# Router weights taken out of TensorE and multiplied in by Pool: one change to the last stage of a two-layer attention and mixture-of-experts kernel

## The reference

```
x = x + attention(layernorm(x), ctx)            # 16 heads, 154 keys
x = x + expert_choice_ffn(layernorm(x))         # 8 experts, each takes its 128 best tokens
x = x + masked_attention(layernorm(x), ctx)     # one head, mask over the keys
x = x + moe(layernorm(x))                       # 32 experts of width 64, 8 per token, and a shared one

# moe, with x of T x 128
aff   = sigmoid(x @ Wr + br)                    # T x 32
w     = aff where it is among the token's top 8, else 0; divided by its sum
gate  = silu(x @ Wg[e] + bg[e])                 # 64 units for each expert e
up    = x @ Wu[e] + bu[e]
out   = shared(x) + sum over e of w[:, e] * ((gate * up) @ Wd[e] + bd[e])
```

## Time and profile before

| what | value |
|---|---|
| time, median of 3 runs (lowest to highest) | 245.97 us (245.62 to 246.22) |
| the profiled execution, its own time | 246.02 us |
| span in the trace, first to last instruction | 244.2 us |
| so outside the span | 1.8 us |
| PE busy | 226.9 us (93%) |
| DVE busy | 180.0 us (74%) |
| ACT busy | 132.0 us (54%) |
| POOL busy | 75.1 us (31%) |
| mean granted clock of PE | 0.996 |

### The profile page before, as it was taken

The page is one execution under the profiler, slowest core; times in us unless marked ns, Lnnn a source line. Parts: engine busy times, 40 slices in busy tenths (PEclk is TensorE's granted clock), DMA queues, the critical chain, the costliest instruction groups (busy, mean ns, idle before and its releaser), DMA issues.

```text
span 244.2 us, 3720 instructions
## 1 busy us (share of the span) xinstructions
PE 226.9 (93%) x1238; PEld 157.4 (64%) x1238; DVE 180.0 (74%) x441; ACT 132.0 (54%) x267; POOL 75.1 (31%) x113
## 2 busy tenths in 40 slices
PE   8989999999997888999999998878999999999993
PEld 2446645664555334688688976646888888888871
DVE  2699887671385887898261688899888888888883
ACT  2437667779625930352443767576554554554551
POOL 6234998020412500000391112100354354354000
PEclk9999999999999999999999999999999999999998
DMA  6994000000000000000043000000111211300002
GB/s 220 399 403 155 3 0 1 3 0 0 3 0 0 0 4 1 0 0 3 1 132 86 0 3 1 0 0 3 43 43 43 86 48 43 86 0 0 3 0 86
DMA packets 5144, 11.62 MB, mean 48 GB/s; under 512 B 803, under 2 KB 1923, under 8 KB 4870
## 3 DMA queue, kind: packets, MB, share of 16 engines
q1 hardware_dynamic: 4294, 10.61, 12.9%
q10 hardware_dynamic: 832, 0.78, 1.0%
HBM read 10.87 MB, written 0.52 MB: 47 GB/s over the span
## 4 chain that ended last, share of the span: by engine, by line
PE 74%; DVE 19%; ACT 3%; issue 2%; POOL 1%; DVEq 0%; ACTq 0%; POOLq 0%
PE bank L1916 6%; PE bank L1917 5%; PE bank L1920 5%; PE bank L1414 5%; PE bank L1281 5%; PE bank L1400 4%; DVE att L686 4%; PE bank L1355 4%; PE bank L1766 3%; PE bank L1950 3%; PE bank L1953 3%; PE bank L1307 3%; PE bank L1951 3%; PE bank L1931 3%; PE bank L1753 3%
## 5 line engine op out<-in xcount | busy, mean ns | idle before, releaser
L1221 ACT ACTIVATE arena_d<-bank,bias 128x512 f32<-128x512 f32 x34 | 23.4, 688 | 32.2 <-PE bank L1920 32.2
L872 DVE SCALAR_TENSOR_TENSOR arena_d<-bank,bias,arena_d 128x512 f32<-128x512 f32 x34 | 25.5, 750 | 9.5 <-ACT arena_d L1221 9.3
L546 DVE TENSOR_REDUCE smax<-bank 128x3 f32<-128x462 f32 (+2 forms) x44 | 25.4, 620 | 5.9 <-PE bank L1355 5.6
L451 POOL CAST arena_b<-rec 128x512 fp32r<-128x512 f32 x17 | 13.4, 787 | 46.7 <-PE bank L1953 46.6
L1916 PE MATMUL bank<-arena_b 128*128 128x512 f32 x68 | 26.8, 393 | 0.1
L1920 PE MATMUL bank<-arena_b 128*128 128x512 f32 x68 | 26.6, 391 | 0.0
L1917 PE MATMUL bank<-arena_b 128*128 128x512 f32 x68 | 26.5, 390 | 0.0
L1028 ACT ACTIVATE arena_c<-bank 128x512 f32<-128x512 f32 x40 | 22.6, 597 | 7.1 <-PE bank L1400 3.3
L886 DVE TENSOR_TENSOR arena_a<-arena_d,arena_a 128x512 fp32r<-128x512 f32 x34 | 23.5, 691 | 0.8 <-ACT arena_a L1228 0.7
L1228 ACT CAST arena_a<-arena_d 128x512 fp32r<-128x512 f32 x34 | 20.8, 612 | 3.4 <-DVE arena_d L881 3.1
L881 DVE TENSOR_TENSOR arena_d<-arena_d,bank 128x512 f32<-128x512 f32 x32 | 21.8, 682 | 0.4 <-PE bank L1931 0.3
(11 more groups left out here) (252 smaller groups left out, 490.9 us busy)
## 6 DMA issues: line engine op xcount, KB each, us to landing
rec<-in_rec SPq DMA_DIRECT2D x17, 257.0 KB, 2.6
arena_d<-in_fc SPq DMA_DIRECT2D x1, 2048.0 KB, 10.7
fc<-in_fc SPq DMA_DIRECT2D x1, 2048.0 KB, 15.1
x<-in_x SPq DMA_DIRECT2D x2, 256.0 KB, 4.5
out<-x SPq DMA_DIRECT2D x2, 256.0 KB, 2.0
watt<-in_watt SPq DMA_DIRECT2D x1, 384.0 KB, 4.3
pack<-in_pack ACTq DMA_DIRECT2D x1, 382.0 KB, 6.2
ctx<-in_ctx ACTq DMA_DIRECT2D x2, 154.0 KB, 7.1
```

What stands on the lines that cost most here:

```text
L546: dve.tensor_reduce(dst, src, AX.X, ALU.max).then_inc(Z["max_done"], 1)
L872: dve.scalar_tensor_tensor(to[:, k % 2, :], bank[:, 2 + k % 2, :], bias[:, u % SPLITS, 1:2], sil[:, k % 2, :], ALU.add, ALU.mult).then_inc ...
L1221: act.activation(sil[:, k % 2, :], bank[:, k % 2, :], f, bias=bias[:, STEPS[k][0] % SPLITS, 0:1])\
```

## The change

From step k = 8 on the router weights are no longer laid over the partitions by a matmul. The weights (32 x 512 for each sequence) are copied out of PSUM by ACT (`raw_weights`), stored to a scratch tensor in DRAM by SP, and for each step read back with the two rows broadcast to 64 partitions each (`laid_weights`, ring of six buffers). POOL multiplies the silu output by them, and DVE's `gated` multiplies up by that product and writes the result to a PSUM bank (5 - k%2), from where the high and low parts are taken. `weighted` and `router_weights` are gone from these steps. The splits of records 6 to 16 move from POOL to ACT (`high_cast`) and DVE (`low_part`), records 0 to 5 are split ahead by POOL into six slots; the biases come with the constants. The third row block of the weights `w3` is copied by POOL and no longer by ACT, `down` runs three steps behind and no longer two, its high and low parts have four buffers, and PE's waits in `gate_and_up` are looser.

```diff
-SPLITS = 5
+SPLITS = 6
+LAID_FROM = 8
+LAID_RING = 6
+PARTS_RING = 4
+        def hidden(k):
+            return bank[:, 5 - k % 2, :] if k >= LAID_FROM else hh[:, k % 2, :]
...
         @block.sync
+            def laid_weights(k):
+                u, b = STEPS[k]
+                m = k - LAID_FROM
+                if m >= LAID_RING:
+                    sp.wait_ge(Z["hh_ready"], k - LAID_RING + 1)
+                if m >= 3:
+                    sp.wait_ge(Z["laid_w%d" % (m % 3)], 16 * (m // 3))
+                own = wraw_d[b, 2 * (u - 1):2 * u, None, :].broadcast_to([2, I1, S])
+                sp.dma_start(laid_w[:, m % LAID_RING, :], own).then_inc(Z["laid_w%d" % (m % 3)], 16)
+            for n in range(3, SPLITS + 3):
+                record(n)
+            for b in range(B):
+                sp.wait_ge(Z["wraw_ready"], b + 1)
+                sp.dma_start(wraw_d[b], wraw[:, b * S:(b + 1) * S]).then_inc(Z["stored"], 16)
+            sp.wait_ge(Z["stored"], 16 * B)
+            for k in range(LAID_FROM, NSTEP):
+                if k % 2 == 0 and SPLITS + 3 <= k // 2 + 3 < PAIRS:
+                    record(k // 2 + 3)
+                laid_weights(k)
...
         @block.gpsimd
-            for n in range(SPLITS, PAIRS):
-                split(n)
+            for b in range(B):
+                pool.wait_ge(Z["whi_ready"], b + 1)
+                pool.tensor_copy(w3[2 * E1:3 * E1, b * S:(b + 1) * S], f32(w3[0:E1, b * S:(b + 1) * S])).then_inc(Z["w3_ready"], 1)
+            for k in range(LAID_FROM, NSTEP):
+                m = k - LAID_FROM
+                pool.wait_ge(Z["laid_w%d" % (m % 3)], 16 * (m // 3 + 1))
+                pool.wait_ge(Z["sil_ready"], k + 1)
+                own = laid_w[:, m % LAID_RING, :]
+                pool.tensor_tensor(own, sil[:, k % 2, :], own, ALU.mult).then_inc(Z["silw_ready"], 1)
...
         @block.vector
+                if k >= LAID_FROM:
+                    m = k - LAID_FROM
+                    dve.wait_ge(Z["silw_ready"], m + 1)
+                    dve.wait_ge(Z["hlo_ready"], k - 1)
+                    if m < 2:
+                        dve.wait_ge(Z["hh_ready"], k - 1)
+                    dve.scalar_tensor_tensor(bank[:, 5 - k % 2, :], bank[:, 2 + k % 2, :], bias[:, u, 1:2],
+                                             laid_w[:, m % LAID_RING, :], ALU.add, ALU.mult).then_inc(Z["hh_ready"], 1)
...
+            def low_part(n):
+                dve.wait_ge(Z["cast_ready"], n + 1)
+                dve.tensor_tensor(wlo[:, n % SPLITS, :], rec[:, n % 3, 0:3 * P], f32(whi[:, n % SPLITS, 0:3 * P]), ALU.subtract)\
+                    .then_inc(Z["split_ready"], 1)
...
             for k in range(8, NSTEP):
                 gated(k)
                 low_hidden(k - 1)
-                weighted(k)
+                if k % 2 == 0 and k // 2 + 2 < PAIRS:
+                    low_part(k // 2 + 2)
...
         @block.scalar
+            def raw_weights(b):
+                act.wait_ge(Z["w3_ready"], 2 * (b + 1))
+                act.copy(wraw[:, b * S:(b + 1) * S], bank[0:E1, (4, 7)[b], :]).then_inc(Z["wraw_ready"], 1)
+            def high_cast(n):
+                act.wait_ge(Z["rec_ready%d" % (n % 3)], 16 * (n // 3 + 1))
+                act.wait_ge(Z["down_done"], STEPS.index((n - SPLITS, 1)) + 1)
+                act.copy(whi[:, n % SPLITS, :], rec[:, n % 3, :]).then_inc(Z["cast_ready"], 1)
...
             for k in range(8, NSTEP):
                 silu(k)
                 high_hidden(k - 1)
+                if k % 2 == 0 and k // 2 + 2 < PAIRS:
+                    high_cast(k // 2 + 2)
...
         @block.tensor
+                laid = k >= LAID_FROM + 2
+                if laid:
+                    pe.wait_ge(Z["sil_ready"], k - 1)
+                elif k >= 2:
                     pe.wait_ge(Z["hh_ready"], k - 1)
...
                 for j in range(2):
+                    if laid and j:
+                        pe.wait_ge(Z["hh_ready"], k - 1)
...
             for k in range(8, NSTEP):
                 gate_and_up(k)
-                router_weights(k)
-                down(k - 2)
+                if k > LAID_FROM:
+                    down(k - 3)
+            down(NSTEP - 3)
             down(NSTEP - 2)
```

More of the change, by code:

```diff
@@ L93 @@
                       ("iota", P), ("jf", len(SHIFTS)), ("jg", EXACT + 1), ("cand0", 1), ("bo", D), ("bv", 1),
-                      ("ln_w", 1), ("ln_b", 1), ("bd_s", 1), ("b1", E0 * FT), ("esel", E0), ("row", 1)):
+                      ("ln_w", 1), ("ln_b", 1), ("bd_s", 1), ("b1", E0 * FT), ("esel", E0), ("row", 1), ("biases", 2 * PAIRS)):
     PACK[_name] = (_at, _at + _width)
@@ L149, in build @@
         br_row = rows3[:, E0 * D:]
+        bias = const("biases").rearrange("p (u j) -> p u j", u=PAIRS)
         b1 = const("b1").rearrange("p (e f) -> p e f", e=E0)
@@ L248, in build @@
         rec = sb("rec", [P, 3, REC])
-        bias = sb("bias", [P, SPLITS, 2])
         def f32(ap):
             return ap.bitcast(F32)
-        L = {n: sem("ld_" + n) for n in ("x0", "x1", "ctx2", "watt", "pack", "late", "rows", "gate", "fc1", "fc2", "mask", "wout", "wr", "bd")}
+        L = {n: sem("ld_" + n) for n in ("x0", "x1", "ctx2", "watt", "pack", "late", "rows", "gate", "fc1", "fc2", "wout", "wr", "bd")}
         names = """var_ready rstd_ready consts_ready xn_ready xnT_psum xnT_ready q_psum qhi_ready qlo_ready k_psum
@@ L319, in _ @@
             sp.dma_start(fc2[:, :, :, :], fc2_d).then_inc(L["fc2"], 16)
-            sp.dma_start(mask[:, :, :], mask_d).then_inc(L["mask"], 16)
+            sp.dma_start(mask[:, :, :], mask_d).then_inc(L["rows"], 16)
             sp.dma_start(wout[:, :, :], wout_d).then_inc(L["wout"], 16)
@@ L329, in _, with record @@
                 sp.dma_start(rec[:, n, :], rec_d[n]).then_inc(Z["rec_ready%d" % n], 16)
-            for n in range(3, PAIRS):
+            def record(n):
                 sp.wait_ge(Z["split_ready"], n - 2)
                 sp.dma_start(rec[:, n % 3, :], rec_d[n]).then_inc(Z["rec_ready%d" % (n % 3)], 16)
+            def laid_weights(k):
[17 more added lines that the diff above has]
+                laid_weights(k)
             for b in range(B):
@@ L392, in _ @@
                 expand(cc)
-            pool.wait_ge(L["mask"], 16)
+            pool.wait_ge(L["rows"], 64)
             pool.tensor_scalar(maskneg[:, :, :], mask[:, :, :], MASKED, 0.0, ALU.mult, ALU.add).then_inc(Z["maskneg_ready"], 1)
@@ L398, in _ @@
                                ALU.add).then_inc(Z["xbo_ready"], 1)
-            pool.wait_ge(L["rows"], 48)
+            pool.wait_ge(L["rows"], 64)
             pool.tensor_copy(rows3[:, :], rows[:, :]).then_inc(Z["rows_split"], 1)
@@ L1225, in high_hidden @@
                 act.wait_ge(Z["hh_ready"], k + 1)
[L1226 to L1228 removed]
+                if k >= PARTS_RING:
+                    act.wait_ge(Z["down_done"], k - PARTS_RING + 1)
+                act.copy(hhi[:, k % PARTS_RING, :], hidden(k)).then_inc(Z["hhi_ready"], 1)
             def result(b):
@@ L1254, in _ @@
             affinities(1)
-            high_weights_again(0)
+            raw_weights(0)
             silu(2)
@@ L1261, in _ @@
             silu(4)
-            high_weights_again(1)
+            raw_weights(1)
             high_hidden(3)
@@ L2076 @@
     rec[0, 0:I1, 2 * P:3 * P] = i["L1_ffn_Wd_s"]
-    rec[0, 0:I1, GW] = i["L1_ffn_bg_s"]
-    rec[0, 0:I1, GW + 1] = i["L1_ffn_bu_s"]
+    biases = np.zeros((P, PAIRS, 2), np.float32)
+    biases[0:I1, 0, 0] = i["L1_ffn_bg_s"]
+    biases[0:I1, 0, 1] = i["L1_ffn_bu_s"]
     n = PAIRS - 1
@@ L2082 @@
     rec[1:, :, 2 * P:3 * P] = i["L1_ffn_Wd"].reshape(n, P, D)
-    rec[1:, :, GW] = i["L1_ffn_bg"].reshape(n, P)
-    rec[1:, :, GW + 1] = i["L1_ffn_bu"].reshape(n, P)
+    biases[:, 1:, 0] = i["L1_ffn_bg"].reshape(n, P).T
+    biases[:, 1:, 1] = i["L1_ffn_bu"].reshape(n, P).T
+    parts = {**consts, **vectors, "biases": biases.reshape(P, 2 * PAIRS)}
     arrays = {
@@ L2105 @@
     out = nc.dram_tensor("out_0", (P, T, D), F32, kind="ExternalOutput").ap()
-    build(nc, *args, out)
+    scratch = nc.dram_tensor("scratch", (B, E1, S), F32).ap()
+    build(nc, *args, scratch, out)
     r = run(nc, [arrays], core_ids=[0])
```

69 lines of the change are left out of this document (33 added, 36 removed).

## The result

The changed kernel takes 331.8 us (median of 4 runs, 331.62 to 332.19) against 245.81 (245.62 to 246.22) before: a ratio of 1.349, 95% interval 1.348 to 1.351. The forecast was 257.4, 249.5 to 259.5. The direction was right and the size far off: 86 us more, not 11.4.

The account below looks back on a forecast made before the run. PE was taken to bound the loop before, and a chain of waits after: 246.02 us plus (6.0 - 4.58) for the first pair, 10 x 1.00 for the others and 0 for the end gave 257.4, range 249.5 to 259.5.

Parts of the forecast that it names:

- Costed at nothing: Ramp, POOL's sixth split ahead and the weight transfers: all expected hidden, adding 0 us; first broadcast 2.6 us.
- The ring of six: Broadcast buffers in the loop: expected to keep transfers ahead, three per pair of rounds in over 5 us.
- signs of being wrong: In the changed profile: even rounds 4.1 us apart with PE fully busy, L932 0.56 long, or POOL waiting for `laid_w`.
- the clock falls or a transfer is late: Rival for the loop: at the lower clock a pair takes 8.2 us, the kernel over 280; chance 0.04, over 260.
- The chain closes on itself: In the loop each even `gate_and_up` waits, through every engine, on the one two rounds earlier; eleven pairs, +11.4 us.
- Pairs: Two loop rounds from an even `gate_and_up` to the next: 5.58 us against 4.58 before, the first pair 6.0.
- silu to POOL: Hand-over in the loop before POOL's product: POOL wakes 0.08 us after the end of what it waited for.
- POOL to DVE: Hand-over in the loop from POOL's product to DVE's `gated`: 0.03 us.
- `low_part` is blocked wholly: On DVE in even rounds, held until 0.14 us before POOL's product ends; pair 5.58 us, 255 to 259, chance 0.66.
- half speed: Rival: `low_part` and POOL's product share SBUF access at half speed; pair 5.33 us, kernel 254.9, chance 0.12.
- no disturbance: Rival: `low_part` reads beside POOL undisturbed; pairs of 4.95 us, kernel 250.1, 248 to 251, chance 0.13.
- The first rival: The wait chain does not bind and PE runs nine matmuls back to back; 240.0 us, chance 0.05.

Follow-up runs that it names:

- e1: Changed kernel with each broadcast load issued as two transfers of one row each; 258.01 us, ratio 1.050 to the kernel before.
- e4: Changed kernel with loads as they were and only the record splits (`low_part`, ACT's cast) one round earlier; 331.64 us, ratio 1.3495.
- f2: As e4, but the scratch holds every row twice, so one load reads 4 rows of 32 repeats; 263.01 us, ratio 1.071.
- e2: As e1, with the split of each later record one round earlier, in the odd rounds; 241.61 us, ratio 0.983.
- e3: As e1, with `low_part` ahead of `low_hidden` on DVE in even rounds; 257.76 us, ratio 1.049.
- g2: As e1, with splits a whole pair of rounds ahead and `low_part` back on POOL behind the odd round's product; 240.49 us, ratio 0.979.

## Why the prediction was wrong

**The step that failed** is "Costed at nothing", its part on the transfers. It put the first broadcast at 2.6 us from issue to landing and let "a pair of rounds" move "three transfers of that size in over 5 us", from the one row of a record load. The bytes alone were taken for the price. The record load has 128 rows of its own, the broadcast two, and the row at 0.13 of 16 engines shows two at work. A broadcast costs 5.35 us alone and 5.64 with its share of a record, so two of them and a record take over 11 us a pair, where the forecast gave the pair 5.58. The ring of six does not help, as the rate is short and not the start. The step's own last sentence then came true: POOL, DVE and PE wait for the whole delay. So did two of its signs of being wrong: POOL waits for `laid_w`, and L932 is 0.55 long. Of the 86.0 us, mending the loads alone takes away 73.8 (331.8 less e1's 258.0) and leaves 12.2; while the loads are slow those 12.2 do not add up with them, as e4 shows.

The Trainium skill, DMA: Bandwidth & Descriptors, section "Why a DMA increments its semaphore by 16 and not by 1", says how many DMA engines a transfer gets: the largest number up to 16 that divides the slowest dimension larger than one on both sides. That makes 2 for this load, 4 for f2's and 16 for e1's. The runs agree: 2.1 engines in the stretch, 5.63 us a product with two rows and 2.92 with four, loads that land in 3.0 us in e1, and small packets that fit 2, 4 and 16. I had not weighed this rule, though the diff has the sizes: the record load of 2.6 us has a first dimension of 128, the broadcast one of 2.

**The rivals.** The case that came is in the last one, "the clock falls or a transfer is late", at 0.04, "over 260". I gave it a price for the clock and none for the transfer: with 26 loads at the 5.64 measured it is 26 x 5.64 = 147 us for the loop, where ten matmuls a round had taken 26 x 2.29 = 60.

**The clock** fell too, to means of 0.83 and 0.66 of full speed in the stretches of the loop above, where PE works between waits of up to 5.5 us; e1 and f2, with shorter waits, have 1.00 in 200 to 210. So in the loop it fell with the late loads, and it is not the cause of the time: in the eight executions of this kernel and of e4 the mean clock goes from 0.851 to 0.897, and the time stays within 0.9 us. The 0.88 of the stretch 160 to 170 is another matter: it is a fall to 0.50 from 160 to 162, before the first broadcast is issued at 170.4, and e2 has the same fall there, e4 none. Why it comes stays open. At the end, where the granted clock is 0.50 (the lower level, 1.2 GHz), 10.9 us pass from the last product's start against 9.2 in e1 (247.6 to 256.8). I put the 1.7 us down to the clock; no run shows that by itself.

**What held**, once the loads are out of the way (e1, 258.0 for 257.4):
- The chain closes on itself, and PE waits at the first matmul of even rounds, eleven times. Pairs are 5.70 (56.96 over ten of them, 182.64 to 239.60), forecast 5.58; the first is 5.73, forecast 6.0. Of the 0.1, silu to POOL is 0.14 where I took 0.08 from the earlier trace rows, and the product 1.27 to 1.30 where I took 1.25.
- POOL to DVE is 0.19 (214.32 to 214.51), not 0.03 as in the earlier trace rows. In e1 that is hidden, since POOL's end decides; in e3's layout it cost the order.
- `low_part` is blocked wholly, as weighed at 0.66 against half speed at 0.12 and no disturbance at 0.13. The Trainium skill, SBUF — State Buffer, section "Who interferes with whom", has this rule; 1.57 us for an operation of 0.55 in e3 agrees with it.
- `gated` into PSUM takes 0.67 to the next start, 0.66 forecast.
- The first rival, the chain not binding, was priced 246.0 - 6.0 = 240.0. g2, where it doesn't bind, has 240.49: the matmul that the change takes away is worth about what the subtraction says, though no run takes it away alone.

That e1 comes within 0.6 us of the forecast is not luck, as the wait, its eleven times and the period are the ones forecast; but a little was mis-sized either way, the pairs up and the first one down.

What stays open: e1's loads were not timed one by one on an idle queue, so their 3.0 us holds for loads issued four at a time within 2.4 us, behind a record. And whether one transfer whose dimensions are laid the other way would do as well as two was not tried.

## What to carry to other kernels

Price a transfer by its form before its bytes: look at the outermost dimension of both sides, and where a broadcast leaves a 2 there, split it into transfers whose outermost dimension is large. A prefetch ring hides a transfer's delay but not its rate, so compare the time of all transfers of a period with the period. When an operation with two SBUF inputs moves to DVE while an operation of POOL with SBUF inputs runs, count it as POOL's remaining time plus its own, and take it off the path or leave it on POOL at a point where its inputs have long been there.

## What the hardware showed

- A load of 256 KB with two rows as its source moved 49 GB/s on 2.1 of 16 DMA engines, and with four rows a product came every 2.92 us and no longer 5.63; as two transfers of 128 KB the same bytes landed 3.0 us after issue.
- DVE's 384 columns took 0.55 us alone and 1.57 when they started 0.12 us into POOL's product of 1.27; POOL's product, which was there first, stayed at 1.27 to 1.30. In e2 the next product, which started 0.24 us before such a blocked operation ended, took 1.40.
- An operation of POOL of 1.3 us was followed by DVE 0.19 us later, one of 1.01 by 0.03: a hand-over taken from one pair of operations did not hold for another.
